# Cross attention in a Perceiver block: the sums of P and V in adjacent pairs, and P's latents transposed and copied apart

## The reference

```python
xn = _ln(x, g_x, b_x)                 # context, 512 rows a batch
ln = _ln(latents, g_l, b_l)           # 64 latents a batch
q = ln @ w_q
kv_in = jnp.concatenate([xn, ln], axis=1)
k, v = jnp.split(kv_in @ w_kv, 2, axis=-1)
q, k, v = (split(q) * scale, split(k), split(v))
sim = jnp.einsum('bhid,bhjd->bhij', q, k)
attn = jax.nn.softmax(sim, axis=-1)
out = jnp.einsum('bhij,bhjd->bhid', attn, v)
```

## Time and profile before

| what | value |
|---|---|
| median of 3 runs | 991.51 us (989.93 to 992.14) |
| span of the profiled execution | 989.7 us |
| PE busy | 960.0 us, 97% of the span |
| DVE busy | 771.2 us, 78% |
| ACT busy | 440.9 us, 45% |
| the 16 batches of cross attention | about 93 to 642 us |

### The profile page before, as it was taken

The page is one execution under the profiler, slowest core; times in us unless marked ns, Lnnn a source line. Parts: engine busy times, 40 slices in busy tenths (PEclk is TensorE's granted clock), DMA queues, the critical chain, the costliest instruction groups (busy, mean ns, idle before and its releaser), DMA issues.

```text
span 989.7 us, 16658 instructions
## 1 busy us (share of the span) xinstructions
PE 960.0 (97%) x6400; PEld 782.6 (79%) x6400; DVE 771.2 (78%) x1652; ACT 440.9 (45%) x848; POOL 129.4 (13%) x140
## 2 busy tenths in 40 slices
PE   9999899999999999999999999999999999999997
PEld 7778788788788787887878888777676778888885
DVE  6545678789788888887887884568888588999985
ACT  4533654664565466447546653633333322222221
POOL 6320000111110110100101010023223000000000
PEclk9999999999999999999999999999999999999999
DMA  6788476676866686676657457071002950000000
GB/s 216 200 257 185 152 150 152 150 126 170 177 115 170 148 162 130 179 139 159 126 144 182 94 175 166 19 196 50 1 2 63 268 137 12 11 11 12 12 12 22
DMA packets 119452, 120.06 MB, mean 121 GB/s; under 512 B 47431, under 2 KB 88071, under 8 KB 117325
## 3 DMA queue, kind: packets, MB, share of 16 engines
q1 hardware_dynamic: 111980, 93.30, 35.1%
q0 software_dynamic: 6816, 24.64, 14.2%
q10 hardware_dynamic: 576, 1.05, 0.3%
HBM read 89.04 MB, written 29.93 MB: 120 GB/s over the span
## 4 chain that ended last, share of the span: by engine, by line
PE 70%; DVE 12%; DMA 5%; issue 5%; ACT 4%; POOL 2%; SPq 1%; another core or an unknown queue 0%; DVEq 0%; ACTq 0%; POOLq 0%
PE ps_banks L147 18%; PE ps_banks L149 17%; PE ps_banks L148 17%; PE ps_banks L466 5%; PE ps_banks L590 3%; PE ps_banks L671 3%; DMA scratch_rstd<-sb_rstd_b 3%; PE ps_banks L738 2%; PE ps_banks L739 2%; PE ps_banks L740 2%; SPq L132 1%; DVE sb_kfull L905 1%; DVE sb_kT_lo L876 1%; DMA sb_w_out_raw<-in_w_out 1%; ACT sb_v L1514 1%
## 5 line engine op out<-in xcount | busy, mean ns | idle before, releaser
L1438 ACT ACTIVATE sb_kT_hi<-sb_kfull 128x512 fp32r<-128x512 f32 x64 | 40.5, 632 | 163.9 <-DVE sb_kfull L905 163.9
L147 PE MATMUL ps_banks<-sb_zT_hi,sb_wkv_hi 128*128 128x512 f32 x256 | 106.1, 415 | 0.6 <-DVE sb_kfull L905 0.6
L148 PE MATMUL ps_banks<-sb_wkv_lo,sb_zT_hi 128*128 128x512 f32 x256 | 100.6, 393 | 0.0
L149 PE MATMUL ps_banks<-sb_zT_hi,sb_wkv_lo 128*128 128x512 f32 x256 | 100.4, 392 | 0.0
L147 PE MATMUL ps_banks<-sb_wkv_hi,sb_zT_hi 128*128 128x512 f32 x256 | 100.4, 392 | 0.0
L149 PE MATMUL ps_banks<-sb_wkv_hi,sb_zT_lo 128*128 128x512 f32 x256 | 100.2, 391 | 0.0
L148 PE MATMUL ps_banks<-sb_zT_lo,sb_wkv_hi 128*128 128x512 f32 x256 | 99.9, 390 | 0.0
L956 DVE CUSTOM_DVE_ANT_0 sb_probs<-ps_banks,sb_maskbias 128x576 f32<-128x576 f32 x64 | 48.1, 752 | 36.8 <-PE ps_banks L149 36.3
L147 PE MATMUL ps_banks<-sb_wgu,sb_z_hi 128*128 128x512 f32 (+1 forms) x192 | 73.8, 384 | 0.0
L148 PE MATMUL ps_banks<-sb_wgu,sb_z_hi 128*128 128x512 f32 (+1 forms) x192 | 72.1, 376 | 0.0
L149 PE MATMUL ps_banks<-sb_wgu,sb_z_lo 128*128 128x512 f32 (+1 forms) x192 | 72.0, 375 | 0.0
(11 more groups left out here) (266 smaller groups left out, 2428.4 us busy)
## 6 DMA issues: line engine op xcount, KB each, us to landing
sb_ctx<-in_ctx SPq DMA_DIRECT2D x16, 1024.0 KB
sb_ctxT<-in_ctx_t SPq DMA_DIRECT2D x16, 1024.0 KB, 7.6
scratch_wgu<-sb_w_both POOLq DMA_DIRECT2D x22, 512.0 KB
sb_wgu<-scratch_wgu SPq DMA_DIRECT2D x44, 256.0 KB, 4.9
sb_wdn<-scratch_wdn SPq DMA_DIRECT2D x8, 704.0 KB, 7.8
scratch_q<-sb_a_qk POOLq DMA_DIRECT2D x8, 512.0 KB, 7.0
sb_rstd_row<-scratch_rstd SPq DMA_DIRECT2D x16, 256.0 KB, 4.8
sb_qpack<-scratch_q SPq DMA_DIRECT2D x32, 128.0 KB, 8.2
```

Of the source, the lines that this page charges most:

```text
L147: e.matmul(o, wh, xh, start=i == 0, stop=False)
L148: e.matmul(o, wh, xl, start=False, stop=False)
L149: m = e.matmul(o, wl, xh, start=False, stop=i == n - 1)
L1438: e.activation(dst, src, ACT.Identity).then_inc(done)
```

## The change

`weigh_v` runs in pairs: for pairs 0 and 1 in slot 0 of the next batch, and for pairs 2 and 3 in slot 3 (slot 2 behind the last batch). The lone transpose of the latents is a function of its own. That of pair 2 comes right ahead of the first pair in slot 0, behind the four transposes, which now stand ahead of `weigh_v`. That of pair 3 moves from slot 1 to slot 3, right ahead of the second pair. ACT's copy of it is a function of its own too and moves to slot 3. For pair 3, `weigh_v` takes the latents last instead of first, so that it waits for that copy only there. Number and size of the instructions are the same.

```diff
             def weigh_v(b, n):
                 i, j = b % 2, n % 2
+                order = (*range(CS), CS) if n == C - 1 else (CS, *range(CS))
                 on.wait_ge(drained[took["p", b, n][0]], took["p", b, n][1])
-                on.wait_ge(drained[took["pt", b, n][0]], took["pt", b, n][1])
                 on.wait_ge(shift_v_landed, 32)
                 if b:
                     on.wait_ge(attn_copied, b)
-                for k in (CS, *range(CS)):
-                    if k < CS:
-                        on.wait_ge(drained[took["v", b, k][0]], took["v", b, k][1])
+                for k in order:
+                    part = ("v", b, k) if k < CS else ("pt", b, n)
+                    on.wait_ge(drained[took[part][0]], took[part][1])
                     for h, r in enumerate(HEAD_ROWS):
                         vs = slice((2 * n + h) * DH, (2 * n + h + 1) * DH)
                         value = vl_pack[i][:, vs] if k == CS else v_sb[i][:, k, vs]
-                        m = e.matmul(o_space(r, n), value, p_t[j][:, k, r], start=k == CS, stop=k == CS - 1)
+                        m = e.matmul(o_space(r, n), value, p_t[j][:, k, r], start=k == order[0], stop=k == order[-1])
                 m.then_inc(v_weighed)
...
+                last_pair = 3 if cur else 2
                 for slot in range(8):
-                    if old and slot < 4:
-                        weigh_v(b - 1, slot)
                     if old and slot < 2:
                         transpose_p(b - 1, slot + 2)
+                    if old and slot == 0:
+                        transpose_p_latents(b - 1, 2)
+                        weigh_v(b - 1, 0)
+                        weigh_v(b - 1, 1)
+                    if old and slot == (last_pair if cur else 1):
+                        transpose_p_latents(b - 1, 3)
+                    if old and slot == last_pair:
+                        weigh_v(b - 1, 2)
+                        weigh_v(b - 1, 3)
                     if cur and slot >= 6:
                         transpose_p(b, slot - 6)
+                        transpose_p_latents(b, slot - 6)
...
                     if old and slot < 2:
                         copy_p(b - 1, slot + 2)
+                    if old and slot == 0:
+                        copy_p_latents(b - 1, 2)
+                    if old and slot == (3 if cur else 1):
+                        copy_p_latents(b - 1, 3)
                     if cur and slot >= 6:
                         copy_p(b, slot - 6)
+                        copy_p_latents(b, slot - 6)
```

More of the change, by code:

```diff
@@ L573, in transpose_p, with transpose_p_latents @@
                 transposes(bank, [probs[j][:, chunk(b, k)] for k in range(CS)]).then_inc(filled[bank])
+            def transpose_p_latents(b, n):
                 bank = claim(("pt", b, n))
-                e.transpose(psum[0:LQ, bank, 0:P], probs[j][:, chunk(b, CS)], ident[:, :]).then_inc(filled[bank])
+                e.transpose(psum[0:LQ, bank, 0:P], probs[n % 2][:, chunk(b, CS)], ident[:, :]).then_inc(filled[bank])
             def weigh_v(b, n):
                 i, j = b % 2, n % 2
+                order = (*range(CS), CS) if n == C - 1 else (CS, *range(CS))
                 on.wait_ge(drained[took["p", b, n][0]], took["p", b, n][1])
-                on.wait_ge(drained[took["pt", b, n][0]], took["pt", b, n][1])
                 on.wait_ge(shift_v_landed, 32)
@@ L1533, in copy_p, with copy_p_latents @@
                 copy(p_t[j][:, 0:CS, :].rearrange("p c n -> p (c n)"), psum[:, bank, :], drained[bank])
+            def copy_p_latents(b, n):
                 bank = taken(("pt", b, n))
-                copy(p_t[j][0:LQ, CS, :], psum[0:LQ, bank, 0:P], drained[bank])
+                copy(p_t[n % 2][0:LQ, CS, :], psum[0:LQ, bank, 0:P], drained[bank])
             def copy_attn(b):
```

## The result

The changed kernel takes 1021.22 us (median of 4 runs, 1019.64 to 1026.98) against 991.47 us before (4 runs, 989.93 to 992.14): a ratio of 1.0305, 95% interval 1.0279 to 1.0332. The prediction said slower, 1005 with 993 to 1014 as the range. The direction was right, and the size was not: +30 us where +13.6 was worked out.

A forecast was written before the change was run, and what follows sets the result against it. PE's own instructions were taken to bound the kernel (busy 97%). +9.6 us for spacing, stops and give-back plus +4.0 for the clock made +13.6 on 989.7, 1003.3; with 1.8 from profile to runs, 1005 us, range 993 to 1014.

The forecast's parts named there:

- PE's spacing as the price of each piece: Slots 0 to 3 on PE: start-to-start distances price the pieces, changes +0.65, -0.99, -0.93, +0.71, sum -0.56 us a batch.
- the rival in which pairing saves nothing: Slots 0 and 3: weight loads pulled ahead hide the tile change, so pairs save nothing; 1010 us, 4% chance.
- The 3.0 us of the `copy_v` stop: Slot 0, odd batches: transposes ahead of `weigh_v` cover PE's stop, -0.37 us in eight batches, -3.0 us.
- The new stop: Slot 3: PE waits for ACT's copy of pair 3's latents, 15 times, 20 to 30 us in all.
- +1.5 holds for batches 1 to 10: +7.5: The net +1.5 us per pair of batches, worked out on batches 9 and 10, carried over to batches 1 to 10.
- This moves only with the slot 4 of the batch before, about +0.1: Batch 10: DVE's `scale_k` waits in slot 0 for the row of rstd, so the change shifts it only about +0.1 us.
- 27.5: Slot 3: the 15 stops on ACT's copy, with the weight load each lays bare, about +27.5 us in all.
- The clock: Behind slot 3's long stops PE falls to half clock; half of five even batches at 1.6 us each, +4.0 us.
- its bound of +11: Upper bound of the half-clock term behind slot 3: 1.6 us in all seven even batches, +11 us.
- Give-back: Slot 6, even batches: PE no longer stops for the output tile's split; 1.25 us back in five batches, -6.25.
- Slots 0 to 2: PE's own work and the stops ending there: 15 times 0.65 - 0.99 - 0.93, and the `copy_v` 3.0; -22.0 us.
- the +13.9 of the forecast's column: All the forecast's terms for batches 1 to 15 added up; 0.3 over its stated 13.6, which rounds some batches.

The follow-up runs named there:

- experiments 1 and 3: Changed kernel with pair 3's lone transpose and its copy back in slot 1: 0.9927; the same with only the first pair adjacent: 0.9952.
- experiment 4: Kernel before, with only slot 0's five transposes put ahead of `weigh_v` and nothing paired: 982.23 us, 0.9971.
- experiment 2: Changed kernel, PE's order untouched, with only ACT's copy of pair 3's latents put ahead of slot 2's `hi_of_k`: 980.55 us, 0.9955.
- experiment 7: Changed kernel with DVE's `scale_k` of slot 2 put first in its slot, ahead of weight steps and statistics: 992.58 us, 1.0080.
- the first control: The changed kernel unaltered, run again on a later chip beside the kernel before: 1004.09 us, 1.0184.
- the first comparison: The original measurement of the unaltered changed kernel against the kernel before: 1021.22 against 991.47 us, 1.0305.
- the controls: The changed kernel unaltered, run twice more beside the kernel before: 1004.09 us (1.0184) and 1002.58 us (1.0200), the latter beside the second filler run.
- experiment 11: Store of the row of rstd delayed 2 us by extra POOL powers: changed kernel 1.0284, kernel before 1.0042, pairs with lone transpose and copy in slot 1 0.9995.
- experiments 6, 7, 8 and 11: Changed kernel with, in turn: ACT's copy ahead of `hi_of_weight` (1.0109), `scale_k` first in slot 2 (1.0080), row of rstd earlier (1.0080), its store 2 us later (1.0284).
- both filler profiles: Changed kernel with eight unused 128-column matmuls on constants ahead of pair 3's latents, run twice: 1005.41 us (1.0205) and 1004.04 us (1.0196).

## Why the prediction came out as it did

**What held.** PE's spacing as the price of each piece, and with it that pairs save 0.33 us: the rival in which pairing saves nothing falls with experiments 1 and 3 (a pair takes 1.53 us, two apart take 1.86). The 3.0 us of the `copy_v` stop (experiment 4). The new stop, its place, its releaser and its count; that ACT's order makes it (experiment 2) and DVE's lag at `scale_k` sizes it (experiment 7). The Trainium skill (TensorE: Matmul & The Clock Gate, Step-by-step: what each phase is for) has the next weight load pulled ahead of the running matmul. It doesn't hide the change of tile in these runs: from start to start, going in takes 0.32 us where the step is 0.23, and two lone groups cost 1.86 us where a pair costs 1.53.

**Which step failed.** "Other even batches are less late (the row of rstd sets it) but give back less, so +1.5 holds for batches 1 to 10: +7.5." Batches 1 to 10 came to +23.0, clock included, 6.8 of it in batches 3 and 4 and 7.6 in batches 5 and 6. For batch 10, from which the step was carried over, its premise "This moves only with the slot 4 of the batch before, about +0.1" held: `scale_k` of slot 0 is 1.64 us behind PE, where the forecast has 1.5. But in batches 4, 6, 8 and 14 it is 2.9, 2.7, 2.4 and 2.1 us behind (1.5, 0.7, 1.1 and 0.4 in the first control), and each time it starts 0.08 us after the row has landed. I took how late the row is from one execution as a property of the kernel. It differs between executions, and the changed kernel passes it on whole: a late row delays DVE's slot 0, that stays to slot 2, and PE stands there for it. In the first comparison rows landed 1.2 to 1.5 us later than in the controls in even batches and about 1 us later in odd ones (`scale_k` of batch 9 started 0.52 us late by it), and the stops with their restart reached 32.9 us in place of 27.5. Rows 5 to 7 us earlier took 9.5 us off; a store 2 us later added 8 to 10.

**The clock** was right as a mechanism and mis-sized, +11.2 in place of +4.0. I counted half of the five longest even stops. It fell behind seven, odd ones among them, and behind one for twice as long. This hangs on the same step, as longer stops bring more of it: with the row early it never fell behind slot 3, and in the controls it cost 5.2 and 4.3 us. The Trainium skill (TensorE: Matmul & The Clock Gate, HAM oscillation — how this bites in real kernels) warns of idle gaps repeated in a loop; by that, the forecast said, its bound of +11 would be the value. These runs agree in part: the first comparison's sum is there, but two of its seven even batches kept 2.4 GHz, and the controls have less than half of it.

**A stop that I didn't see.** The transpose of slot 1 claims a bank whose weight is drained late. In batch 4:

```profile
231.75 0.63 PE L466 MATMUL ps_banks<-sb_ident,sb_probs 128*128 128x128 f32 x4 [1.40 <-DVE sb_w_both L887]
```

ACT had been held before it by the store of the weight before:

```profile
230.28 0.60 ACT L1449 ACTIVATE sb_w_both<-ps_banks 128x512 fp32r<-128x512 f32 x1 [4.45 <-DMA scratch_wgu<-sb_w_both]
```

With the spacing around it this is worth 2.7 us in four batches. Neither control shows it (slot 1 is -0.99 there in all even batches). It came back in part, 1.1 us, with the row delayed, and 2.3 us of it in experiment 7. So it appears where DVE or the weight's store is late, and not with the change alone; which of the two it takes was not tested.

**Give-back.** -3.4 in place of -6.25. I had let five even batches give back 1.25 each, as batch 10 would. The row itself says that this can't be: the five stops for the split tile are 3.5 us in all. Batches 2, 8 and 10 gave back 0.9 to 1.2 each, batches 4 and 6 only 0.2, which is about what their stops had been.

Together: 5.4 for the stops, 7.2 for the clock, 2.7 for the new stop, 2.9 not given back and 0.1 in slot 3's own pieces are 18.3. Slots 0 to 2 did 2.6 better: stops of the kernel before in batches 7 and 12 ended (2.1 us), and projections ran 0.5 us closer. That leaves 15.7, as between +29.6 and the +13.9 of the forecast's column. The 2.1 us aren't a gain of the change: the kernel before in experiment 11 has these stops no more either.

**What stays open.** With the row late in both, the change costs 2.4%; the first comparison has 3.05%. The other 0.6%, little more than the intervals of the runs, may be what else was late there: the rows of odd batches, which the delay did not make late, and the weights' stores of slot 1. Neither was tried by itself. Why the way from store to landing was longer there isn't known. And beside the controls the change costs 18 to 19 us where the forecast says 13.6; no profile of the kernel before was taken with them, so these 5 us aren't divided among the terms.

## What to carry to other kernels

An instruction that PE needs must not stand, in the order of the engine that makes it, behind one that waits for a slower chain, however idle that engine is: the copy took 0.25 us on an engine 56% idle and made PE stop for 29 us; put ahead of one instruction it left 0.2 us. Move the consumers together, if their spacing saves something, but leave the producers where they were.

A price read from one execution is a price at that execution's memory timing. Ask what absorbs a late transfer now, and whether the change takes that slack away. Here it did: a store 2 us later cost 8 to 10 us, and 4 before. The opposite cost nothing that the runs show: statistics finished in slot 3 instead of 4 won 5 to 6 us even where nothing waited in slot 3.

## What the runs showed of the hardware that I had not expected

- The granted clock isn't a function of the stop's length. Over seven profiles (the changed kernel three times, experiments 6, 7, 8 and 11) PE stopped 105 times right behind the transposes and the 36 small matmuls. Behind 23 of the 30 stops of 1.7 us or more it fell to 1.2 GHz in the projection that followed. Behind none of the 75 shorter ones it did. A stop of 3.16 us passed at 2.4 GHz, one of 1.70 did not. What decides between them isn't settled.
- Matmuls on constants in place of the idle time kept 2.4 GHz behind slot 3 in all 15 batches of both filler profiles (mean clock 0.997 to 0.998 in the four runs of the second, against 0.986 to 0.993 in its control).
- The changed kernel, the same program, differed by 1.7 to 1.9% between the first comparison and the later ones, where the kernel before differed by 0.7%.
